# Sixteen-step transformer stack on one core: the last layer's two attentions and the cluster mix work several batches in different phases at once, and layer norm statistics are taken in the stage ahead

## The chip, the cores and the metric

The kernel runs on one core of one Trainium2 chip. The metric is the device time of one execution, in microseconds. Before the change the median of three runs is 6564.3 us (6562.81 to 6569.73).

## The reference, cut to what matters

A float32 tensor `x` of 16 sequences ("batches") of 256 tokens by 128 features passes through sixteen residual steps, `x = x + f(layernorm(x))`. The ones whose loops are rewritten:

```python
def _L3_attn_a_ref(x, q_w, kv_w, proj_w, proj_b):      # 16 heads of 8, windows of 32 tokens, one shared k and v
    q = x @ q_w.T
    k, v = split(x @ kv_w.T)                           # 8 features each
    attn = softmax(q_window @ k_window.T * 8 ** -0.5)  # per head and window: 32 x 32
    return (attn @ v_window) @ proj_w.T + proj_b

def _L3_attn_b_ref(x, Wq, bq, Wk, bk, Wv, bv, Wo, bo, g1, be1, W1, b1, W2, b2, g2, be2):
    q, k, v = heads(Wq, bq), heads(Wk, bk), heads(Wv, bv)
    qn, kn = elu(q) / norm(elu(q)), elu(k) / norm(elu(k))
    ctx = qn @ (kn.T @ v) / sqrt(8)                    # per head: an 8 x 8 state
    attn_out = layernorm(ctx @ Wo + bo + x, g1, be1)
    return layernorm(gelu(attn_out @ W1 + b1) @ W2 + b2 + attn_out, g2, be2)

def _L2_ffn_ref(x, ...):                               # used twice; its last part is the "mix"
    tile_idx = ...                                     # one of 64 rows of a table, for each token
    comp = tanh(gelu(x @ compress_w1 + compress_b1) @ compress_w2 + compress_b2)
    hh = relu(comp[:, 0:1] * w1a[tile_idx] + comp[:, 1:2] * w1b[tile_idx] + b1[tile_idx])
    mag = sum(hh * w2[tile_idx]) + b2[tile_idx]
    return layernorm(x + mag * directions[tile_idx] * output_scale) * norm_gamma + norm_beta
```

The order of the sixteen steps is: l0_attn_a, l0_ffn, l0_attn_b, l0_ffn, l1_attn_a, l1_ffn, l1_attn_b, l1_ffn, l2_attn_a, l2_ffn, l2_attn_b, l2_ffn, l3_attn_a, l3_ffn, l3_attn_b, l3_ffn.

## The kernel before, in words

`X` (the residual, 32 tiles of 128 tokens by 128) and `XNT` (the layer norm's output, features on the partitions) stay in SBUF. Each step is one or more blocks; all engines meet at the end of a block. Inside a block every engine runs its own program in order, and the programs wait for one another by counting semaphores (`wait_ge`, `then_inc`). A wait stops everything that is queued behind it on its engine. `drain()` makes VectorE wait for its own earlier writes.

Every step begins with `layer_norm`: VectorE takes `bn_stats` of all 32 tiles (line 193), combines them (lines 196 to 205), ScalarE takes a root, and then rows are scaled (line 216), turned by TensorE (line 240) and copied to `XNT` by ScalarE (line 265). Nothing else goes on in the block while the statistics are taken.

The attentions and the mix loop over pairs of batches, and each engine does phase after phase, both batches of the pair in each phase:

- `l3_attn_a` (lines 1385 to 1548): ScalarE copies the batch's slice of XNT (L1484); TensorE projects k and q (L1425, L1426); VectorE repeats the slice four times (L1515) for the product that gives v (L1431); VectorE masks v (L1521) and makes sixteen masked copies of k, one for each head (L1526); TensorE makes the scores (L1442); VectorE takes the maximum and subtracts it (L1533, L1535); ScalarE takes exp (L1493); VectorE sums, inverts and scales the probabilities (L1539, L1541, L1543); TensorE turns them (L1450), ScalarE copies them out (L1497), TensorE multiplies by v (L1459), and output copies (L1501, L1505), a second turn (L1466) and the last projection (L1468, L1473) follow; VectorE adds to X (L1548).
- `l3_attn_b` (lines 1168 to 1382): the same kind of chain: projection (L1224), bias and elu on VectorE with exp on ScalarE (L1332 to L1341), norms (L1343 to L1352, the root at L1295), the state (L1235, L1357), context (L1242), output projection on y1 (L1245 to L1252), first normalising (L830, L833, L1317, L1321, with a power on GpSimd), turn (L1259), the wide layer (L1266) with gelu (L1311), the second projection on y2 (L1270 to L1276), second normalising and the add to X (L1321 to L1382).
- the mix of `l2_ffn` (lines 2590 to 2701): ScalarE copies the one-hot rows (L2635), TensorE turns them (L2608) and starts the compression (L2609), ScalarE copies and takes gelu (L2639, L2643), TensorE picks the table's rows (L2615) and compresses (L2617, L2622), ScalarE takes tanh (L2647), and VectorE does all the rest (L2671 to L2701). ScalarE starts the next pair only when VectorE has added the last one to X (the semaphore `done`).

In `load_all` (lines 99 to 124) the first block ends only when six DMAs that fill `slots_x` in HBM with zeros have landed. In `sparse_experts` rows go out to HBM and come back by indirect DMAs on GpSimd's queue (L551, L559), and VectorE adds each returned tile to X (L492).

## Time and profile before

| | |
|---|---|
| median of three runs | 6564.3 us (6562.81 to 6569.73) |
| the profiled execution's own time | 6556.34 us |
| its span, first to last instruction | 6554.4 us |
| TensorE busy (matmul) | 3941.5 us, 60% |
| VectorE busy | 3888.1 us, 59% |
| ScalarE busy | 2334.7 us, 36% |
| GpSimd busy | 1684.8 us, 26% |
| mean granted TensorE clock | 0.78 of full speed |
| DMA | 26 GB/s over the span |

Busy is the share of the span in which an engine executes something; a granted clock of 0.50 is 1.2 GHz and 1.00 is 2.4 GHz, and a value between is a stretch that had both. No engine is near full, so the time lies in the waits of one engine for another, and those must be read stage by stage.

### The profile page before, as it was taken

The page shows a single profiled execution, that of the slowest core. Times are in us where ns is not written, and L with a number is a line of the kernel's source. Part 1 is how long each engine was busy: PE and PEld are TensorE (multiplying, and loading weights), DVE is VectorE, ACT ScalarE, POOL GpSimd, SP SyncE. Part 2 cuts the span into 40 slices and gives each one's busy share as a digit, 9 for nine tenths or more (in the row PEclk, how much of TensorE's full clock was granted, in tenths as well). Part 3 has the DMA queues.
Part 4 walks back from the last instruction along what each step waited for, and adds up shares of the span by engine and source line. Part 5 has one row for each costly group of instructions (what it writes and reads, how often), then busy time and mean ns, then how long its engine had stood idle before and what let it go on. Part 6 is the DMA issues. An engine that isn't in the chain of part 4 may idle for free. (4 is left out here: it accounts for less than half of the span.)

```text
span 6554.4 us, 78028 instructions
## 1 busy us (share of the span) xinstructions
PE 3941.5 (60%) x21844; PEld 2462.1 (38%) x21844; DVE 3888.1 (59%) x7406; ACT 2334.7 (36%) x4114; POOL 1684.8 (26%) x1639
## 2 busy tenths in 40 slices
PE   5756539366734688445666634888536647456474
PEld 3555429122223233231222222444324446444364
DVE  3334644599963777437888865555656635455354
ACT  2322214355512477224544432333322224233242
POOL 0043023455523355232433320000000041200402
PEclk8767659688867899676878865999756679777798
DMA  2012002000002222030000000000000011100111
GB/s 78 1 53 69 0 23 82 30 0 0 0 4 66 85 88 64 4 95 12 0 0 0 0 2 17 0 0 0 1 3 0 1 42 41 42 0 2 42 39 49
DMA packets 224792, 170.38 MB, mean 26 GB/s; under 512 B 27371, under 2 KB 211538, under 8 KB 223650
## 3 DMA queue, kind: packets, MB, share of 16 engines
q1 hardware_dynamic: 204066, 125.44, 6.5%
q0 software_dynamic: 20480, 41.98, 2.2%
q8 instruction: 114, 1.87, 0.1%
q14 instruction: 132, 1.08, 0.1%
HBM read 92.02 MB, written 74.45 MB: 25 GB/s over the span
## 5 line engine op out<-in xcount | busy, mean ns | idle before, releaser
L1630 POOL TENSOR_TENSOR XN<-s_l_attn_a_h,LOG 128x512 f32<-128x512 f32 x512 | 641.9, 1275 | 770.7 <-DVE s_l_attn_a_h L1670 754.2
L1670 DVE TENSOR_TENSOR_SCAN s_l_attn_a_h<-s_l_attn_a_da,XN 128x512 f32<-128x512 f32 x512 | 598.4, 1210 | 138.7 <-ACT s_l_attn_a_da L1615 98.5
L1606 PE MATMUL s_l_attn_a_y_ps<-XN,c_ident 128*128 128x512 f32 x1024 | 588.2, 703 | 24.4 <-DVE s_l_attn_a_y L1882 15.0
L613 PE MATMUL s_l_ffn_ffn_down<-down,s_l_ffn_ffn_hid 128*128 x2944 | 425.0, 285 | 206.6 <-DVE s_l_ffn_ffn_hid L485 184.1
L1615 ACT ACTIVATE s_l_attn_a_da<-s_l_attn_a_delta,s_l_attn_a_a 128x510 f32<-128x510 f32 x512 | 353.3, 690 | 526.9 <-DVE s_l_attn_a_h L1670 526.4
L559 POOL DMA_INDIRECT s_l_ffn_ffn_back<-slots_y,s_l_ffn_ffn_slots x320 | 303.0, 947 | 911.9 <-DMA slots_y<-PICK 617.3
L613 PEld LDWEIGHTS s_l_ffn_ffn_down<-down,s_l_ffn_ffn_hid 128*128 128x128 f32 x2944 | 362.3, 192 | 255.5 <-issue 253.8
L472 DVE COPY s_l_ffn_ffn_xt<-s_l_ffn_ffn_turned 128x128 f32<-128x128 f32 x416 | 121.0, 291 | 549.0 <-PE s_l_ffn_ffn_turned L594 547.2
L1585 PE MATMUL s_l_attn_a_spread<-s_l_attn_a_parts,s_l_attn_a_pick 96*128 96x512 bf16 x512 | 182.0, 442 | 388.7 <-DVE XN L1661 237.6
L605 PE MATMUL s_l_ffn_ffn_up<-s_l_ffn_ffn_xt,s_l_ffn_ffn_own_w 128*128 128x128 f32 x2944 | 410.7, 281 | 8.1 <-DVE s_l_ffn_ffn_own_w L405 4.8
L229 POOL COPY XN<-s_l_ffn_ln_rows 128x512 f32 x64 | 40.9, 638 | 1455.0 <-DVE s_l_ffn_ln_rows L216 1455.0
L551 POOL DMA_INDIRECT slots_x<-XN,s_l_ffn_ffn_slots x320 | 313.1, 978 | 390.1 <-DVE s_l_ffn_ffn_slots L449 294.4
L3154 DVE TENSOR_REDUCE s_l_attn_b_top<-s_l_attn_b_m_ps 128x2 f32<-128x512 f32 x512 | 330.0, 687 | 89.7 <-PE s_l_attn_b_m_ps L2860 85.6
L605 PEld LDWEIGHTS s_l_ffn_ffn_up<-s_l_ffn_ffn_xt,s_l_ffn_ffn_own_w 128*128 128x128 f32 x2944 | 370.3, 196 | 17.4 <-issue 11.2
L1606 PEld LDWEIGHTS s_l_attn_a_y_ps<-XN,c_ident 128*128 128x128 f32 x1024 | 224.6, 226 | 286.9 <-issue 235.7
L1661 DVE TENSOR_TENSOR XN<-s_l_attn_a_dx,s_l_attn_a_spread 128x1024 f32<-128x1024 f32 x256 | 306.0, 1195 | 6.4 <-PE s_l_attn_a_spread L1585 3.7
L3024 ACT ACTIVATE s_l_attn_b_e<-s_l_attn_b_s_ps 128x512 f32<-128x512 f32 x512 | 284.8, 604 | 40.1 <-PE s_l_attn_b_s_ps L2873 33.6
L594 PE MATMUL s_l_ffn_ffn_turned<-c_ident,XNT 128*128 128x128 f32 x416 | 115.5, 281 | 277.2 <-DMA XNT<-slots_x 277.2
L535 ACT ACTIVATE s_l_ffn_ffn_silu<-s_l_ffn_ffn_shifted_a 128x512 f32<-128x512 f32 x160 | 100.8, 630 | 482.0 <-DVE s_l_ffn_ffn_shifted_a L480 482.0
L1585 PEld LDWEIGHTS s_l_attn_a_spread<-s_l_attn_a_parts,s_l_attn_a_pick 96*128 96x128 bf16 x512 | 37.9, 102 | 615.2 <-DVE XN L1661 386.7
L539 ACT ACTIVATE s_l_ffn_ffn_hid<-s_l_ffn_ffn_up 128x512 f32<-128x512 f32 (+1 forms) x256 | 132.5, 518 | 346.8 <-PE s_l_ffn_ffn_up L605 346.1
L492 DVE SCALAR_TENSOR_TENSOR X<-s_l_ffn_ffn_back,s_l_ffn_ffn_gates,X 128x128 f32<-128x128 f32 x320 | 111.5, 350 | 204.3 <-DMA s_l_ffn_ffn_back<-slots_y,s_l_ffn_ffn_slots 198.3
(629 smaller groups left out, 8785.9 us busy)
## 6 DMA issues: line engine op xcount, KB each, us to landing
XNT<-slots_x SPq DMA_DIRECT2D x32, 640.0 KB, 6.0
slots_y<-LOG SPq DMA_DIRECT2D x16, 640.0 KB, 4.3
slots_y<-PICK SPq DMA_DIRECT2D x16, 640.0 KB, 4.3
s_l_attn_b_qr<-s_l_attn_b_q_rows SPq DMA_DIRECT2D x64, 144.0 KB
s_l_attn_b_kr<-s_l_attn_b_k_rows SPq DMA_DIRECT2D x64, 144.0 KB
XNT<-slots_x SPq DMA_DIRECT2D x8, 768.0 KB, 6.1
slots_x<-XN,s_l_ffn_ffn_slots POOLq DMA_INDIRECT x320, 2.2
s_l_ffn_ffn_back<-slots_y,s_l_ffn_ffn_slots POOLq DMA_INDIRECT x320, 2.5
```

Source lines behind the costliest of these rows:

```text
L551: nc.gpsimd.indirect_dma_start(k.slots_x[h][0:NH * P, :], bass.IndirectOffsetOnAxis(slots[:, c, t:t + 1], 0), k.XN[:, t, :], None).then_in ...
L559: nc.gpsimd.indirect_dma_start(back[:, n % 8, :], None, k.slots_y[h][0:NH * P, :], bass.IndirectOffsetOnAxis(slots[:, c, t:t + 1], 0)).the ...
L605: last = nc.tensor.matmul(out[:, c % chunks, :], own_w1[j % 3][:, c * P:(c + 1) * P], xt[j % 3][:], start=True, stop=True)
L613: last = nc.tensor.matmul(down[j % 2][:], hid[j % 3][:, c, :], w2[:, bass.ds(first + c * D, D)], start=(c == 0), stop=(c == chunks - 1))
L1585: last = self.nc.tensor.matmul(self.spread[:, i, :], self.pick[:, i * NST + n:i * NST + n + 1].to_broadcast([96, P]), self.parts[par][:], ...
L1606: last = self.nc.tensor.matmul(self.y_ps[:, i, :], self.k.ident[:], self.hc[n % 2][:, i, :], start=(n == 0), stop=(n == NST - 1))
L1615: self.nc.scalar.activation(self.da[:, i, :, 1:], self.delta[par][:, i, :].rearrange("p (b t) -> p b t", b=BPG)[:, :, 1:], ACT.Exp, scale= ...
L1630: self.nc.gpsimd.tensor_tensor(self.hc[n % 2][:, i, :], self.h[n % 2][:, i, :], self.c_rows[n % 2], ALU.mult).then_inc(self.hc_ready, 1)
L1661: self.nc.vector.tensor_tensor(self.u[n % 2], self.dx[par][:], b, ALU.mult).then_inc(self.u_ready, 1)
L1670: self.nc.vector.tensor_tensor_scan(self.h[n % 2][:, i, :], self.da[:, i, :, :].rearrange("p b t -> p (b t)"), self.u[n % 2][:, i, :], 0.0 ...
L3024: nc.scalar.activation(e[h][:], s_ps[BANK[n * H + h]][:], ACT.Exp, scale=HD ** -0.5).then_inc(e_ready, 1)
L3154: nc.vector.tensor_reduce(top[n % 2][:, :, h % 2, h // 2], m_ps[BANK[n * H + h]][:], AX.X, ALU.max).then_inc(max_ready, 1)
```

## The change

- `l3_attn_a`: one batch in each step instead of two, and in a step each engine works on up to four batches in different phases: batch i+2 is projected and its keys masked, batch i+1 is scored, shifted and exponentiated, batch i is turned, multiplied by v and turned back, batch i-1 is projected out and added. Each phase has a PSUM bank of its own. Eight of the sixteen masked key copies move to ScalarE; the four repeated copies move to GpSimd; probabilities are no longer scaled, the 128x256 output is divided instead (and ScalarE's copy of it goes away). A few steps ahead of the loop and behind it are written out (19 steps in all).
- `l3_attn_b`: a step does the first half (to the context) of one pair and the second half (from the output projection) of the pair before it, interleaved on each engine; 9 steps, the first and the last half empty. The residual's slice is copied once more (`xr`). `hid_ps` and `proj` are single banks or bank pairs shared by the two batches.
- The mix: front buffers in a ring of four; ScalarE waits for `rows_used` (VectorE's last read of the ring slot, four batches back) instead of `done`. The table is laid out by GpSimd with zeros so that one 128-row product picks each tile's rows.
- Statistics: `bn_stats` of a tile is taken right after its add to X in l0_attn_a, l0_attn_b, l2_attn_b and the three expert steps; the eight layer norms behind those steps skip line 193.
- Load: ten smaller fills, and the block no longer waits for them; GpSimd waits ahead of the first scatter.

```diff
@@ load_all
+                for first in range(0, 40, fill_tiles):          # fill_tiles = 8
+                    ...
+                    sp.dma_start(dst, ...).then_inc(k.slots_filled, 16)
-            sp.wait_ge(loaded, n + 16 + 6 * 16)
+            sp.wait_ge(loaded, n + 16)
+def take_stats(nc, dve, k, first, count):
+    dve.drain()
+    for t in range(count):
+        nc.vector.bn_stats(flat(k.stats[:, bass.ds(first + t, 1), :]), tile(k.X, first + t))
@@ layer_norm
+            if not stats_taken:
+                for t in range(TILES):
+                    nc.vector.bn_stats(stats[:, t, :], k.X[:, t, :])
+                dve.drain()
@@ sparse_experts, combine
+                if c == choices - 1:
+                    dve.drain()
+                    nc.vector.bn_stats(k.stats[:, t, :], k.X[:, t, :])
@@ sparse_experts, gpsimd
+            pool.wait_ge(k.slots_filled, k.fills)
@@ l0_attn_a and l0_attn_b, after each pair; l2_attn_b, after each group of four tiles
+                take_stats(nc, dve, k, pair * (2 * TPB), 2 * TPB)
@@ l3_attn_b, tensor
+            def step(a, b):
+                project(a, 0)
+                first_out(b, 0); first_out(b + 1, 1)
+                project(a + 1, 1)
+                turn_rows(b, 0); turn_rows(b + 1, 1)
+                go_up(b, 0)
+                turn_and_add_up(a, 0)
+                go_down(b, 0)
+                turn_and_add_up(a + 1, 1)
+                go_up(b + 1, 1)
+                apply_state(a, 0); apply_state(a + 1, 1)
+                go_down(b + 1, 1)
@@ l3_attn_b, vector
+            def step(a, b):
+                add_bias(a, 0)
+                variance(b, 0, 0, y1_ready); variance(b + 1, 1, 0, y1_ready)
+                add_bias(a + 1, 1)
+                normalise(b, 0, 0); normalise(b + 1, 1, 0)
+                square(a, 0); square(a + 1, 1); scale(a, 0); scale(a + 1, 1)
+                mask_state(a, 0); mask_state(a + 1, 1)
+                variance(b, 0, 1, y2_ready); variance(b + 1, 1, 1, y2_ready)
+                finish(b, 0); finish(b + 1, 1)
@@ l3_attn_b, scalar
+            def step(a, b):
+                keep_x(a, 0); keep_x(a + 1, 1); exponents(a, 0); exponents(a + 1, 1)
+                keep_rows(b, 0); keep_rows(b + 1, 1)
+                roots(a, 0); roots(a + 1, 1)
+                middle(b, 0)
+                keep_qt(a, 0); keep_qt(a + 1, 1); keep_residual(a, 0); keep_residual(a + 1, 1)
+                middle(b + 1, 1)
+                keep_ctx(a, 0); keep_ctx(a + 1, 1)
@@ l3_attn_a
+            tensor: turn_probs(i), project(i+2), project_out(i-1), score(i+1), mix(i), project_v(i+1), turn_out(i)
+            scalar: copy pt(i), keep_kq(i+2) with 8 key copies, keep_x(i+3), exp(i+1), copy ot(i)
+            vector: add_up(i), mask_keys(i+2) (8 copies), add_out(i-1), shift(i+1), divide(i), keep_v(i+1)
+            gpsimd: repeat(u+1) after v_up(u)
@@ l2_ffn mix
+        RING = 4
-                    act.wait_ge(done, u + 1)
+                        act.wait_ge(rows_used, u + 1)
-                        last = nc.tensor.matmul(row_ps[m][:, t, 0:TW], pt[m][r:r + NT, :], w["L2f_table"][r:r + NT, :], start=True, stop=True)
+                            last = nc.tensor.matmul(row_ps[m][:, t, 0:TW], pt[m][:], table[:, t, :], start=True, stop=True)
```

(The `step` lists of l3_attn_a are written here as one line for each engine; in l3_attn_b the conditions that leave out a or b in the first and last step are left out.)

## Rows read from the trace of the kernel before

**Rows 1.** Windows of five loops: length, busy us of each engine, clock, DMA, GB/s.

```profile
3897.00:4048.00 151.00, 59.89 (x208) 35.50 (x208) 76.35 (x304) 38.11 (x80) 11.38 (x16) 0.50 0.00 0
4754.00:4905.00 151.00, 56.57 (x208) 32.67 (x208) 76.68 (x304) 38.10 (x80) 11.35 (x16) 0.52 0.01 2
4926.00:5204.00 278.00, 175.38 (x1856) 116.38 (x1856) 175.50 (x432) 71.21 (x120) 0.00 (x0) 0.70 0.00 0
5412.00:5500.00 88.00, 62.99 (x518) 59.09 (x518) 45.24 (x84) 36.47 (x63) 0.00 (x0) 1.00 0.12 33
5733.00:6038.00 305.00, 179.40 (x864) 134.15 (x864) 152.60 (x416) 97.31 (x184) 22.40 (x33) 0.77 0.00 0
```

**Rows 2.** Timeline of l3_attn_a, one pair: start, length, engine, line, [idle before, releaser].

```profile
4968.88 8.48 DVE L1526 TENSOR_SCALAR s_l_attn_a_keys<-s_l_attn_a_kk,s_l_attn_a_c_head_of_row 128x256 f32<-128x256 f32 x32
4973.31 3.43 PE L1442 MATMUL s_l_attn_a_big_a<-s_l_attn_a_keys,s_l_attn_a_q 128*32 128x512 f32 x16 [4.80 <-DVE s_l_attn_a_keys L1526]
...
4977.51 1.92 PE L1442 MATMUL s_l_attn_a_big_a<-s_l_attn_a_keys,s_l_attn_a_q 128*32 128x512 f32 x16 [0.77 <-DVE s_l_attn_a_keys L1526]
...
4979.83 1.06 ACT L1493 ACTIVATE s_l_attn_a_p<-s_l_attn_a_p 128x1024 f32<-128x1024 f32 x1 [10.64 <-DVE s_l_attn_a_p L1535]
...
4985.14 1.97 PE L1450 MATMUL s_l_attn_a_big_b<-c_ident,s_l_attn_a_p 128*128 128x128 f32 x8 [5.71 <-DVE s_l_attn_a_p L1543]
...
4987.14 1.01 ACT L1497 COPY s_l_attn_a_pt<-s_l_attn_a_big_b 128x1024 f32<-128x1024 f32 x1 [3.82 <-PE s_l_attn_a_big_b L1450]
```

**Rows 3.** Groups by line, VectorE in l3_attn_a's loop: busy us, mean ns, idle before.

```profile
L1543 DVE TENSOR_TENSOR s_l_attn_a_p<-s_l_attn_a_p,s_l_attn_a_den 128x1024 f32<-128x1024 f32 x16 | 19.6, 1225 | 1.2
...
L1515 DVE COPY s_l_attn_a_xrep<-s_l_attn_a_xg 128x256 f32<-128x256 f32 x64 | 13.6, 286 | 5.8 <-ACT s_l_attn_a_xg L1484 5.2 <-issue 0.6
```

**Rows 4.** Timeline of l3_attn_b, one pair.

```profile
5807.45 0.49 DVE L830 BATCH_NORM_STATS2 s_l_attn_b_stats<-s_l_attn_b_late 128x6 f32<-128x128 f32 x2 [3.72 <-PE s_l_attn_b_late L1276]
...
5829.77 0.50 DVE L830 BATCH_NORM_STATS2 s_l_attn_b_stats<-s_l_attn_b_late 128x6 f32<-128x128 f32 x2 [4.00 <-PE s_l_attn_b_late L1252]
...
5840.18 0.50 DVE L830 BATCH_NORM_STATS2 s_l_attn_b_stats<-s_l_attn_b_late 128x6 f32<-128x128 f32 x2 [6.85 <-PE s_l_attn_b_late L1276]
...
5841.05 1.70 ACT L1311 ACTIVATE s_l_attn_b_hid<-s_l_attn_b_proj,s_l_attn_b_L3b_b 128x256 f32<-128x256 f32 x4 [2.62 <-PE s_l_attn_b_proj L1266]
...
5844.96 0.49 DVE L830 BATCH_NORM_STATS2 s_l_attn_b_stats<-s_l_attn_b_late 128x6 f32<-128x128 f32 x2 [3.72 <-PE s_l_attn_b_late L1276]
```

**Rows 5.** Timeline of the first mix, VectorE, first pair and start of the second.

```profile
3905.62 0.29 DVE L2671 TENSOR_TENSOR s_l_ffn_mix_sp<-s_l_ffn_mix_row_ps,s_l_ffn_mix_comp 128x32 f32<-128x32 f32 x2 [14.01 <-ACT s_l_ffn_mix_comp L2647]
...
3917.49 0.42 DVE L2701 TENSOR_TENSOR X<-X,s_l_ffn_mix_y 128x256 f32 x1
...
3924.55 0.29 DVE L2671 TENSOR_TENSOR s_l_ffn_mix_sp<-s_l_ffn_mix_row_ps,s_l_ffn_mix_comp 128x32 f32<-128x32 f32 x2 [6.63 <-ACT s_l_ffn_mix_comp L2647]
```

**Rows 6.** Timeline: statistics, and what VectorE does where they will be taken.

```profile
4905.36 6.29 DVE L193 BATCH_NORM_STATS2 s_l_attn_a_ln_stats<-X 128x6 f32<-128x128 f32 x32 [0.32 <-PEq L47]
...
253.94 0.96 DVE L962 TENSOR_TENSOR s_l_attn_a_qkv<-s_l_attn_a_proj,s_l_attn_a_L0a_bqkv 128x768 f32<-128x768 f32 x1 [1.06 <-PE s_l_attn_a_proj L880]
...
628.67 0.35 DVE L492 SCALAR_TENSOR_TENSOR X<-s_l_ffn_ffn_back,s_l_ffn_ffn_gates,X 128x128 f32<-128x128 f32 x1 [0.96 <-DMA s_l_ffn_ffn_back<-slots_y,s_l_ffn_ffn_slots]
...
4609.85 1.21 DVE L2405 TENSOR_TENSOR s_l_attn_b_swap<-s_l_attn_b_sw_ps,s_l_attn_b_c_sin 64x1024 f32<-64x1024 f32 x1
```

**Rows 7.** Timeline of the load block: the fills' issue, the next issue.

```profile
5.42 15.99 SPq L117 DMA_DIRECT2D slots_x<-PICK  x6
26.50 0.34 SPq L138 DMA_DIRECT2D up<-in_L_ffn_w  x1
```

**Rows 8.** Groups by line in layer norms, with and without GpSimd's copy beside them.

```profile
L216 DVE TENSOR_SCALAR s_l_ffn_ln_rows<-X,s_l_ffn_ln_meanvar,s_l_ffn_ln_rstd 128x128 f32 x32 | 10.4, 386 | 6.2 <-ACTq L260 5.5 <-issue 0.6
...
L216 DVE TENSOR_SCALAR s_l_attn_a_ln_rows<-X,s_l_attn_a_ln_meanvar,s_l_attn_a_ln_rstd 128x128 f32 x32 | 8.7, 342 | 1.7 <-ACTq L260 1.2 <-issue 0.5
...
L229 POOL COPY XN<-s_l_ffn_ln_rows 128x512 f32 x8 | 5.1, 642 | 323.2 <-DVE s_l_ffn_ln_rows L216 323.2
```

More of the change, by code:

```diff
@@ L1191, in l3_attn_b @@
[L1191 to L1194 removed]
+        proj, hid_ps = s.ps("proj", [P, TPB, 512]), s.ps("hid_ps", [P, CH, SEQ])
+        mid, late = s.two_ps("mid", [P, 512]), s.two_ps("late", [P, 512])
@@ L1200, in l3_attn_b, with over_phases, since @@
         block = s.block()
+        def over_phases(engine, step):
+            step(0, None)
+            with engine.Fori(0, PAIRS - 1) as pair:
+                step(pair * 2 + 2, pair * 2)
+            step(None, BATCH - 2)
+        def since(engine, sem, count):
+            if not isinstance(count, int) or count > 0:
+                engine.wait_ge(sem, count)
         @block.gpsimd
@@ new lines, in l3_attn_a, with has, over_batches @@
+        turned_o, ot_ready, y_up, added = s.sem("turned_o"), s.sem("ot_ready"), s.sem("y_up"), s.sem("added")
+        xrep_ready, v_up, vals_ready = s.sem("xrep_ready"), s.sem("v_up"), s.sem("vals_ready")
+        block = s.block()
+        def has(u):
+            return not isinstance(u, int) or 0 <= u < BATCH
+        def over_batches(engine, step):
+            for i in range(-2, 1):
+                step(i, i % 2)
+            with engine.Fori(0, (BATCH - 4) // 2) as pair:
+                step(pair * 2 + 1, 1)
+                step(pair * 2 + 2, 0)
+            for i in range(BATCH - 3, BATCH + 1):
+                step(i, i % 2)
@@ new lines, in score @@
+            def score(u, m):
+                since(pe, shifted, u)
+                pe.wait_ge(q_ready, u + 1)
+                pe.wait_ge(act_keys, u + 1)
+                pe.wait_ge(dve_keys, u + 1)
+                for t in range(TPB):
+                    for i in range(WPT):
+                        n = t * WPT + i
+                        last = nc.tensor.matmul(s_ps[i * WIN:(i + 1) * WIN, t, :], q[m][:, n * WIN:(n + 1) * WIN],
+                                                keys[m][:, n, :, :].rearrange("p h u -> p (h u)"), start=True, stop=True)
+                last.then_inc(scored, 1)
@@ new lines, in _, with repeat @@
+            pe.wait_ge(loaded, 16 * len(names))
+            over_batches(pe, step)
+        @block.gpsimd
+        def _(pool):
+            def repeat(u):
+                since(pool, v_up, u)
+                for h in range(HB):
+                    last = nc.gpsimd.tensor_copy(xrep[:, :, h, :], k.XNT[:, bass.ds(u * SEQ, SEQ)].rearrange("p (n u) -> p n u", u=WIN))
+                last.then_inc(xrep_ready, 1)
+            repeat(0)
+            with pool.Fori(0, BATCH - 1) as u:
+                repeat(u + 1)
@@ L2651, in _ @@
             nc.gpsimd.memset(minus[:], -0.5)
+            nc.gpsimd.memset(table[:], 0.0)
+            pool.drain()
+            pool.wait_ge(loaded, 16 * len(names))
+            for t in range(TPB):
+                r = t * NT
+                last = nc.gpsimd.tensor_copy(table[r:r + NT, t, :], w["L2f_table"][r:r + NT, :])
+            last.then_inc(table_ready, 1)
             pool.drain()
@@ L3367, in build @@
             STEPS[step](nc, k, f"s{n}_{step}")
+            k.stats_taken = step not in ("l3_attn_a", "l2_ffn", "l3_attn_b", "l1_attn_a", "l1_attn_b", "l2_attn_a")
             later = [p for p in plan[n + 1:] if p in experts]
```

812 lines of the change are left out of this document (427 added, 385 removed).

## The prediction, made before the changed kernel was run

> **What bounds the kernel now.** I read the totals first: no engine is busy for more than 60% of the span, so no engine's work is the limit. The chain of waits says little, as it only follows the last expert step. So I cut the span into the loops that the change touches and read windows of them, then one pair of each loop in the timeline. The reader is to see three things. In both mixes VectorE is the busiest engine with 76 us of 151, at a clock of 0.50 [rows 1]. In l3_attn_a TensorE and VectorE are each busy 175 of 278 us, the clock at 0.70; in l3_attn_b 179 and 153 of 305, at 0.77 [rows 1]. And in the timeline these take turns: ScalarE waits 10.64 us for the shift, TensorE 4.80 for the keys and 5.71 for the probabilities [rows 2]; in l3_attn_b VectorE waits 4.00 us for y1, then 6.85 and 3.72 for y2 [rows 4]; in the mix 6.63 us for tanh [rows 5]. All are latencies of a chain with two batches at the same place in it, and they are what several phases at once can fill. The eight layer norms hold VectorE for 6.29 us with nothing beside [rows 6].
>
> **l3_attn_a.** A pair takes 278/8 = 34.8 us, a batch 17.4 [rows 1]. VectorE per batch afterwards: eight key copies at 8.48/32 = 0.265 us = 2.1 (sixteen before) [rows 2]; maximum and subtraction, each of 1024 elements like the 1225 ns row, with overlap and drain 2.5; the sum of 1024 and the reciprocal 1.7; the scaling of 1225 ns goes and a 256-element one of about 0.45 comes; masked v and the add 0.45 each; the repeats (4 x 286 ns, overlapped 0.85) leave [rows 3]. Sum 7.7 us. TensorE at 2.4 GHz: score 1.9 (3.4 at 1.2 GHz), turning eight blocks about 1.2 (the row has 1.97 behind a long wait) [rows 2]; k and q 0.8, v 1.9, times v 1.1, output and second turn 1.2, from the same pair of the timeline: 8.2 us. ScalarE: probabilities out 1.01, exp 1.06 [rows 2], k, q, x and output copies 1.3, table load 0.6 (one in two steps), and eight key copies. A 256-column activation with a per-partition operand is not there as a copy; the nearest is gelu with a bias, four in 1.70 us, 0.43 apart [rows 4]. Bounds are 0.27 and 0.57 apart (2.1 to 4.5 us for eight); I take 0.42, 3.4 us. Sum 7.4 us.
>
> No sum is the step, because the order closes a ring. With t = 0 where exp(i) ends: TensorE turns to 1.4, ScalarE copies out to 2.5 and hands over k at 2.9; VectorE, idle since 1.8, masks keys to 5.1 and adds out to 5.6; TensorE has meanwhile made k, q and the output and ends the score of i+1 at 5.0; the shift runs to 8.1; exp 8.3 to 9.35, and the ring is closed. Product by v (6.1), v's projection (8.0) and divide (8.6) lie beside it. ScalarE's key copies end at 6.7 (7.9 at the upper bound) and are hidden by the shift. So 9.4 us, with the table load and loop ends 9.8. What is late next is VectorE's wait for k, 1.1 us. Fifteen such steps are 147, two steps of filling 15, the last real one 5.5, the one behind it 2: 170 us. The clock will not be full everywhere, 4 us. 278 becomes 174: **-104** (bounds: 9.2 us a step gives -113; 11.5 us, TensorE mostly at 1.2 GHz with 12.6 us of work in some steps, gives -78).
>
> The four repeats go to GpSimd, which has nothing else and works a step ahead, so they are off the ring. Against them stands what a copy on GpSimd does to VectorE beside it: rows scaled in a layer norm take 386 ns beside GpSimd's 642 ns copies and 342 without [rows 8]. On eight key copies that is at most 0.35 us a step, inside the 4 us above and its bound. The Trainium skill ("SBUF — State Buffer", Who interferes with whom) says of this that a VectorE instruction in a two-port mode and a GpSimd instruction exclude each other for their whole length. If key copies fell under it and always came second, four copies of half of 642 ns would stop VectorE for 1.3 us in each of 16 batches, 21 us; the rows show 44 ns, so I don't count it.
>
> **l3_attn_b.** One pair takes 37.5 us (5807.45 to 5844.96) [rows 4]. VectorE's waits in it are 3.72 + 4.00 + 6.85 and 2.0 of small ones, so its work with drains is 21 us. The new step has all that work once. I follow it from the end of the squares, about 11.7 us into a step (two biases 3.8, two variances 1.9, normalising 1.4, two squares 4.3): ScalarE's second root, table load, four gelus of 0.43 [rows 4] take 3.4 us; TensorE, whose order puts the second batch's turn and state behind go_down(b), finishes them at 5.0, so VectorE, which had 3.0 us of work, waits 2.0. Then go_up of the second batch, its gelus behind the qt and residual copies (7.7), two apply_state, go_down (1.7): y2 of the second batch at 10.2, against VectorE ready at 6.4: a wait of 3.8. Then a variance and two finishes, 5.4. Sum 11.7 + 10.2 + 5.4 = 27.3, and the next step's projection is hidden by the finishes. I take 27.7 for the clock. The first step is a's chain alone, 19.5 us, the last b's alone, 22. 19.5 + 22 + 7 x 27.7 = 235 against 305: **-70** (bounds: 26 us a step -82; 31 us -46). The extra copy `xr` and three table loads a step are in ScalarE's 14 us of 27.7. TensorE has 16.6 us at 2.4 GHz. The single `hid_ps` makes go_up(b+1) wait for the first gelus, which the order does anyway.
>
> **The mixes.** VectorE is busy without a gap from 3905.62 to 3917.91, 12.3 us, then waits 6.63 us [rows 5]. With the ring, ScalarE may start a pair when VectorE has read the rows two pairs back, at least 12 us ahead of need, and its chain takes 8.5 us. So the wait goes; VectorE's own 12.1 us (the second pair has 12.0) is late next. 8.6 (first front) + 8 x 12.1 + 2.5 (table layout on GpSimd, loop) = 108 against 151 [rows 1]: **-86** for both (bounds: no lead at all 0; -90). The clock of 0.50 hides in the lead as well.
>
> **Statistics.** 8 x 6.29 us go, less 0.1 each, as the ScalarE table load of 1.28 us beside them now ends last: -49.6 [rows 6]. What comes: 32 bn_stats at 0.197 us again, in other places. In l0_attn_a four and a drain, 0.95 us, against an idle 1.06 [rows 6]: 0.1 a pair, and 0.95 behind the last: 1.8; in l0_attn_b the idle time there is longer, 1. In l2_attn_b nothing stands between the add and the next work, which is on the path (L2405 has no idle time before it) [rows 6]: 8 x 0.95 = 7.6, more than the 6.2 that its successor's norm gives back. In the experts' tail each add waits 0.96 us for a returned tile [rows 6] and the new 0.3 us fits, except the last: 0.35 in each of four; in l1_ffn, where every add has one, I put 1.5 in each of two. The last l3_ffn takes them for nothing. Together +14.8, net **-35** (bounds -25 to -44).
>
> **Load.** The fills' issue on SP's queue, 16 us for the same bytes, stays, and the wait from 21.4 to 26.5 goes [rows 7]: **-4.6** (bounds 0 to -5). Weights issued next lie behind the same transfers, but are wanted 20 us later.
>
> **Sum.** 104 + 70 + 86 + 35 + 5 = 300 off the profiled execution's 6556.3 = 6256. The runs shown have a median 8 us over that execution, so 6264; for handshakes that my schedules leave out I add 6: **6270 us**.
>
> **Rivals.** (1) *The steps are longer than the hand schedule*: TensorE stays at 1.2 GHz for much of the two attentions. For it speaks that the clock is 0.70 and 0.77 now with TensorE busy 63% and 59%; against it that an expert loop with TensorE busy 72% and no wait over 2 us has 1.00 [rows 1]. Price: l3_attn_a steps of 12.6 us (TensorE's work at 1.2 GHz) 15 x 2.8 = 42 more, l3_attn_b steps of 33 us 7 x 5.3 = 37 more: 6350 us. The Trainium skill ("TensorE: Matmul & The Clock Gate", HAM oscillation) says that waits between bursts throw the array back to the lower clock. The waits that I leave in the step are under 3 us where they were 4.8 to 5.7, and by that rule, too, the higher clock is the likelier. (2) *The mix's front doesn't run ahead*, because ScalarE's queue waits for tanh of this pair before it copies the next: 8 chains of 8.5 us still fit into 12.1, so little speaks for it; 86 less gain, 6356. (3) *More than I count*: steps at 9.2 and 26, the norms' -44: 6240, or near 6215 if the copies by ScalarE cost 0.27. (4) *Slower than before*: the in-order queues close the rings so that no two phases overlap, l3_attn_a above all, where a step has one batch and four engines pass it on. One batch's chain alone is 26 us there: 19 x 26 = 494, +216; l3_attn_b 8 x 41.5 = 332, +27; mixes -86, norms -35, load -5: 6680. It decides once a step of l3_attn_a is longer than some 27 us, three times my ring, and nothing in the rows needs that. (5) *It doesn't do what it says* (the norms still take statistics, the loop still in step): within 0.2%, 13 us.
>
> **How the numbers follow.** Forecast 62%, its own range 6235 to 6310; rival 1 and 2 together 22%; rival 3 13%; rival 4 2%; rival 5 1%. The 8-in-10 range takes in rival 1's and 2's price on the slow side and, on the fast side, rival 3's with a little of the unlisted gains: 6205 to 6360. About 0.2% is what a measurement of this kernel can tell from no change. Faster 97%, same 1%, slower 2%.
>
> **What would show it.** Right: loops of about 174 and 235 us and two of 108; ScalarE's exp in l3_attn_a released every 9.8 us; VectorE in the mix with no wait for tanh after the first; a wait of VectorE for y2 near 4 us; line 193 in eight norms only; the clock over 0.85 in both attentions; VectorE's idle time before L2405 gone into bn_stats. Wrong: a step of l3_attn_a over 11.5 us, TensorE the engine without gaps in it, or ScalarE's key copies beyond the end of the shift.

## The result, and the profile after

The changed kernel takes **6264.6 us** (median of four runs, 6253.8 to 6268.7) against 6566.7 for the kernel before in the same session (6562.8 to 6569.7): a ratio of **0.9538**, 95% interval 0.9521 to 0.9554. Its profiled execution took 6263.55 us with a span of 6261.6, 292.8 us less than the one before. The forecast was 6270.

The windows of the loops in the changed kernel, in the order of the two mixes, l3_attn_a and l3_attn_b (columns as in [rows 1]: after the length come the busy times of TensorE, its weight loads, VectorE, ScalarE and GpSimd, then the granted clock):

```profile
3859.50:3964.40 104.90, 59.65 (x208) 39.74 (x208) 76.55 (x304) 27.45 (x72) 12.05 (x18) 0.58 0.00 0
4671.90:4776.80 104.90, 58.40 (x208) 39.27 (x208) 76.48 (x304) 27.48 (x72) 12.02 (x18) 0.60 0.00 0
4798.00:4974.00 176.00, 155.46 (x1856) 108.46 (x1856) 115.69 (x240) 100.74 (x225) 22.86 (x64) 0.81 0.00 1
5496.20:5745.20 249.00, 187.99 (x864) 135.22 (x864) 151.00 (x416) 100.60 (x199) 22.40 (x33) 0.84 0.00 0
```

Against [rows 1] VectorE does the same work in less time in the mixes and in l3_attn_b: it is busy 73% of a mix instead of 51%. In l3_attn_a it has 60 us less to do (115.7 against 175.5), of which 30 came to ScalarE (100.7 against 71.2) and 23 to GpSimd, and TensorE is busy 88% of the loop instead of 63%. The clock came out at 0.81 and 0.84 in the attentions.

To place every microsecond I cut each kernel at the instruction in each norm with which VectorE completes the variance, just ahead of the root (line 205 before, 216 in the changed kernel), so a stage is a step and the statistics of the norm behind it. Microseconds, worked out from the timelines:

```
stage (ends at the next norm's root)     before   after   difference
load and first norm                        35.1    32.5     -2.6
l0_attn_a                                 295.0   282.9    -12.1
l0_attn_b                                 243.6   238.5     -5.1
l0_ffn, twice                       313.8+316.6 307.8+309.2  -13.4
l1_ffn, twice                       262.1+260.9 254.8+256.0  -12.2
l2_attn_b                                 630.4   627.0     -3.4
l1_attn_a, l1_attn_b, l2_attn_a          2098.1  2102.7     +4.6
l2_ffn, twice                       230.9+226.3 187.7+185.5  -84.0
l3_attn_a                                 299.2   197.9   -101.3
l3_attn_b                                 326.9   270.1    -56.8
l3_ffn, twice                       507.1+508.5 500.3+508.8   -6.5
```

One step of l3_attn_a in the timeline of the changed kernel (columns as in [rows 2]):

```profile
4862.95 1.06 ACT L1637 ACTIVATE s_l_attn_a_p<-s_l_attn_a_p 128x1024 f32<-128x1024 f32 x1 [1.84 <-DVE s_l_attn_a_p L1660]
...
4864.06 1.97 PE L1524 MATMUL s_l_attn_a_t_ps<-c_ident,s_l_attn_a_p 128*128 128x128 f32 x8 [0.26 <-ACT s_l_attn_a_p L1637]
...
4866.68 0.85 PE L1533 MATMUL s_l_attn_a_kq_ps<-s_l_attn_a_xg,s_l_attn_a_L3a_wq 128*128 128x256 f32 x2
...
4867.97 2.19 DVE L1651 TENSOR_SCALAR s_l_attn_a_keys<-s_l_attn_a_kk,s_l_attn_a_c_head_of_row 128x256 f32<-128x256 f32 x8 [2.28 <-ACT s_l_attn_a_kk L1620]
...
4868.72 1.93 PE L1552 MATMUL s_l_attn_a_s_ps<-s_l_attn_a_keys,s_l_attn_a_q 128*32 128x512 f32 x16
...
4870.72 1.23 DVE L1658 TENSOR_REDUCE s_l_attn_a_top<-s_l_attn_a_s_ps 128x32 f32<-128x1024 f32 x1 [0.22 <-PE s_l_attn_a_s_ps L1552]
...
4873.27 1.06 ACT L1637 ACTIVATE s_l_attn_a_p<-s_l_attn_a_p 128x1024 f32<-128x1024 f32 x1 [1.83 <-DVE s_l_attn_a_p L1660]
```

From one exp to the next is 10.32 us (10.25 later in the loop). The shift is released by the score and not by VectorE's own masks. The score is released by nothing, it stands behind TensorE's own turn, projection and output. Windows inside this step, of the same kernel, show at which clock (the last column but two):

```profile
4864.00:4866.10 2.10, 2.04 (x9) 2.04 (x10) 1.57 (x2) 0.30 (x3) 0.41 (x2) 0.50 0.00 0
4866.10:4867.60 1.50, 1.50 (x5) 0.87 (x5) 0.00 (x0) 1.01 (x2) 0.00 (x0) 0.64 0.00 0
4867.60:4873.20 5.60, 5.54 (x102) 3.73 (x102) 4.93 (x12) 3.84 (x11) 0.00 (x0) 1.00 0.00 0
4873.20:4874.30 1.10, 0.41 (x2) 0.20 (x2) 0.70 (x3) 1.03 (x2) 0.99 (x3) 0.87 0.00 0
```

The turn and most of k and q run at 1.2 GHz, the rest at 2.4 GHz; the fall comes in the only stretch of the step in which TensorE is mostly idle (0.41 of 1.10 us busy). All steps of the loop but one have such a stretch at 1.2 GHz. The one without it, between the second exp and the third, is 1.6 us shorter than its successor, with the same instructions:

```profile
4822.80:4831.62 8.82, 8.01 (x116) 5.59 (x116) 7.21 (x16) 6.11 (x15) 1.43 (x4) 1.00 0.01 2
4831.62:4842.07 10.45, 9.61 (x116) 6.77 (x116) 7.21 (x16) 6.20 (x14) 1.43 (x4) 0.84 0.01 2
```

VectorE in l3_attn_b, its wait for y2 of the second batch in two full steps, 27.55 us apart, and for y2 of the first batch in the last step; TensorE's wide layer of that step stands ahead of it:

```profile
5602.17 0.50 DVE L845 BATCH_NORM_STATS2 s_l_attn_b_stats<-s_l_attn_b_late 128x6 f32<-128x128 f32 x2 [4.38 <-PE s_l_attn_b_late L1282]
...
5629.72 0.50 DVE L845 BATCH_NORM_STATS2 s_l_attn_b_stats<-s_l_attn_b_late 128x6 f32<-128x128 f32 x2 [4.38 <-PE s_l_attn_b_late L1282]
...
5725.46 3.73 PE L1271 MATMUL s_l_attn_b_hid_ps<-s_l_attn_b_at,s_l_attn_b_L3b_w 128*128 128x256 f32 x8
...
5734.65 0.50 DVE L845 BATCH_NORM_STATS2 s_l_attn_b_stats<-s_l_attn_b_late 128x6 f32<-128x128 f32 x2 [9.72 <-PE s_l_attn_b_late L1282]
```

VectorE in the first mix, the first instruction of the second and of the third pair (the same as in [rows 5], where it waits 6.63 us for tanh):

```profile
3880.26 0.28 DVE L2834 TENSOR_TENSOR s_l_ffn_mix_sp<-s_l_ffn_mix_row_ps,s_l_ffn_mix_comp 128x32 f32<-128x32 f32 x2
...
3892.38 0.29 DVE L2834 TENSOR_TENSOR s_l_ffn_mix_sp<-s_l_ffn_mix_row_ps,s_l_ffn_mix_comp 128x32 f32<-128x32 f32 x2 [0.18 <-issue]
```

The load block, to be compared with [rows 7]; of the 5.1 us between the fills' issue and the next one 0.45 are left:

```profile
5.42 16.14 SPq L118 DMA_DIRECT2D slots_x<-PICK  x10
22.01 1.42 SPq L140 DMA_DIRECT2D up<-in_L_ffn_w  x1
23.48 1.24 SPq L140 DMA_DIRECT2D down<-in_L_ffn_w  x1
25.11 0.34 SPq L197 DMA_DIRECT2D s_l_attn_a_L0a_wqkv<-in_L0a_wqkv  x1
```

### The profile page after: what moved, and what is told of

Read it like the earlier page. It is cut to its first block and busy times, and to the rows that moved or that the text cites. A ratio compares the mean times of both kernels' runs of the same rounds, so it can differ in the third digit from the quotient of the medians.

```text
span 6261.6 us, 78605 instructions
## 1 busy us (share of the span) xinstructions
PE 3935.5 (63%) x21844; PEld 2470.7 (39%) x21844; DVE 3852.3 (62%) x7246; ACT 2346.4 (37%) x4218; POOL 1709.6 (27%) x1709
```

## The experiments

They were measured in four sessions, each with the kernel before beside them. It takes 6566 us in two of them (the record numbers their chips 15 and 6) and 6739 in the other two (numbered 2 and 6). In the changed kernels all of the difference is in the six expert stages (l0_ffn 347 us there against 308), and every other stage agrees within the spread given below. What makes those stages longer isn't shown; the number 6 stands beside both times. So kernels are compared by their ratio to the kernel before in the same session, and by stages, each read from one profiled execution. A ratio of 0.001 is 6.6 us. Stages with unchanged code spread between profiles: l0_attn_a 282.8 to 288.8, l2_attn_a 876 to 894, l3_attn_b 264.5 to 270.1 (ten profiles, mean 266.7).

**All statistics back in the norms.**

```diff
-            k.stats_taken = step not in ("l3_attn_a", "l2_ffn", ...)
+            k.stats_taken = False
-                take_stats(nc, dve, k, ...)      # and the bn_stats in combine
```

> The changed kernel (6264.6 us) with every layer norm taking its own statistics again and none taken in a stage ahead; all else as changed. By the terms of my sum the statistics are worth 35 us: 6300 us. Rival, from the stages compared after the run: the eight stages ahead of these norms got 53 us shorter and three stages whose code is the same 5 us longer, so 48 to 53: 6313 to 6318 us. If the 5 us of the three stages (l1_attn_a, l1_attn_b, l2_attn_a) belong to the statistics too, they must fall back to their times before (1.2, 2.4 and 1.0 us less); if not, they stay.

Ratio 0.9625 (0.9611 to 0.9638): 57 us more than the changed kernel. By stages, against those of the next three kernels (same session) that keep the stage as changed: l0_attn_a +10 (against one of them, and 6 to 12 against the spread), l0_attn_b +5, the five expert stages +5, +5, +9, +5 and +6, l2_attn_b +5, together 50. My 35 is out. l1_attn_a, l1_attn_b and l2_attn_a take 661.4, 563.1 and 876.5 us, 2101.0 together, against 2102.7 in the changed kernel and 2098.1 before. The 4.6 us between those two did not go away with the statistics, and they are smaller than the spread of l2_attn_a alone.

**Statistics of l2_attn_b alone back in the norm.**

```diff
-                take_stats(nc, dve, k, g * GT, GT)
```

> The changed kernel with the statistics of l2_attn_b alone moved back to the norm behind it. By my term they cost 7.6 us in the loop (8 times 0.95, nothing beside) against 6.2 in the norm: the stage gets 1.4 us shorter, 6263 us. Rival: VectorE's next wait for TensorE's swapped product takes the 0.95 us in (6.18 us before, 5.23 after), and only the last of eight is on the path: the stage gets 4 to 5 us longer, 6269 us. The times are within the measurement's bound of each other, so the stage in the profile decides: group period 75.05 us with the statistics out, 75.1 with them in, if the rival holds; 76.0 with them in by my term.

Ratio 0.9554 (0.9538 to 0.9570), which can't tell; the stage took 632.5 us against 626.6 to 627.6 in the others: 5.4 more. The rival holds by the stage. Groups by line over the stage, in the kernel before and then in the changed one, show where the 8 us of statistics went (last column: idle before the line, and what ended it):

```profile
L2405 DVE TENSOR_TENSOR s_l_attn_b_swap<-s_l_attn_b_sw_ps,s_l_attn_b_c_sin 64x1024 f32<-64x1024 f32 x64 | 77.8, 1216 | 156.2 <-PE s_l_attn_b_sw_ps L2315 156.2
```

```profile
L2555 DVE TENSOR_TENSOR s_l_attn_b_swap<-s_l_attn_b_sw_ps,s_l_attn_b_c_sin 64x1024 f32<-64x1024 f32 x64 | 77.8, 1215 | 149.0 <-PE s_l_attn_b_sw_ps L2465 149.0
...
L167 DVE BATCH_NORM_STATS2 LOG<-X (+1 forms) x32 | 8.0, 291 | 1.4 <-issue 1.2
```

In the kernel before, the first L2405 behind the add to X has no wait ([rows 6]), but the next one has 6.18 us. Over the stage 7.2 us of these waits vanished against 8.0 us of new work.

**Statistics of l0_attn_a alone back in the norm, and the same taken twice.**

```diff
 # e7: in l0_attn_a only
-                take_stats(nc, dve, k, pair * (2 * TPB), 2 * TPB)
 # e8: in l0_attn_a only
+                take_stats(nc, dve, k, pair * (2 * TPB), 2 * TPB)
```

> The changed kernel with the statistics of the first attention (l0_attn_a) alone moved back to the norm behind it. By my term: 6.2 more in the norm, 1.8 less in the loop, 6269 us. Rival: the 12.1 us that this stage gained are mostly the clock, which was granted in another rhythm over its eight pairs once each pair was a little longer (30.0, 33.5 and 35.4 us in turn at 0.89, 0.80 and 0.76, where before 33.1 and 35.2 took turns); then the old rhythm comes back and the stage loses some 12 us: 6276 us.

> The changed kernel with the four statistics behind each pair of l0_attn_a taken twice (the second time is waste). If a statistic is simply work on the path, each pair gets 0.87 to 0.95 us longer and nothing else changes: 7 to 7.6 us, 6272 us. Rival: pair lengths follow the clock, and a shift of 0.9 us moves which pairs get the high one: the 30.0, 33.5, 35.4 us rhythm changes to another, and the stage moves by several us in either direction beside the 7: anywhere from 6260 to 6285 us, with at least two pairs over 1.5 us away from where they were.

Without them the ratio is 0.9562 (0.9549 to 0.9575) and the stage 292.9 us. With them twice it is 0.9530 (0.9514 to 0.9545) and the stage **268.0 us**: 0.76 us of waste work in each pair (VectorE busy 13.61 us against 12.85) made the stage 15 us shorter. The ratio of the whole kernel is too coarse to confirm the 15 us: it is 5 us below the changed kernel's, and the intervals overlap. Windows of three pairs of the changed kernel, then of two of the kernel with the statistics twice:

```profile
183.84:213.87 30.03, 21.44 (x97) 15.57 (x96) 12.85 (x25) 11.43 (x21) 0.00 (x0) 0.89 0.00 0
213.87:247.41 33.54, 24.95 (x97) 17.89 (x96) 12.85 (x24) 11.43 (x21) 0.00 (x0) 0.80 0.00 0
247.41:282.84 35.43, 26.84 (x97) 19.50 (x96) 12.86 (x25) 11.43 (x21) 0.00 (x0) 0.76 0.00 0
```

```profile
174.67:205.43 30.76, 21.43 (x97) 15.58 (x96) 13.61 (x29) 11.43 (x21) 0.00 (x0) 0.89 0.00 0
205.43:236.20 30.77, 21.44 (x97) 15.58 (x96) 13.61 (x29) 11.43 (x21) 0.00 (x0) 0.89 0.00 0
```

The same 97 matmuls take 21.4 or 26.8 us. In the changed kernel the granted clock goes through a rhythm over three pairs; with 0.76 us more work in each pair, all seven distances from pair to pair are 30.76 to 30.79 us, and the clock 0.89. Without the statistics five of the seven distances are 33 and 35 us again, as in the kernel before. So the rivals hold on the mechanism in both runs. On the size they don't: without them the stage is 4 to 10 us longer than in the kernels that have them once, not 12, and with them twice it gained more than "several us".

**The mix in step again.**

```diff
-                        act.wait_ge(rows_used, u + 1)
+                        act.wait_ge(done, u + 1)       # done: VectorE's add to X
```

> The changed kernel with one edit in both mixes: ScalarE waits for the add of the batch two back (as before the change) instead of for VectorE's last read of the ring slot four back. Ring, banks and the padded table stay. If the lead is the whole of the gain, each mix gives its 42 us back: two VectorE waits of 6 to 7 us for tanh a pair again, 6348 us. Rival: the front also got shorter or longer by the padded table and the banks of its own; then each mix lands elsewhere than at 151 us, by 8 times the difference of a front (0.4 us of TensorE in a pair: 3 us a mix).

6346.8 us, 0.9664 (0.9650 to 0.9679): 82 more. The two l2_ffn stages took 231.4 and 226.8 us, those of the kernel before 230.9 and 226.3. The lead is the whole gain; ring buffers and the padded table alone give nothing.

**Score first in l3_attn_a; score and shift first.**

```diff
 # TensorE, both
+                if has(i + 1):
+                    score(i + 1, 1 - par)
                 if has(i):
                     turn_probs(i, par)
 ...
-                if has(i + 1):
-                    score(i + 1, 1 - par)
 # VectorE, the second kernel only: shift(i + 1) ahead of add_up(i)
```

> The changed kernel with one edit in l3_attn_a: TensorE makes the scores of batch i+1 first in a step, ahead of turning the probabilities of batch i, of the projection of i+2 and of the output of i-1. Theory: a step is 10.3 us because TensorE's own queue is on the ring (turn 1.97, k and q 1.9, output 1.3, score 1.93), where I had put VectorE's masks there; with the score out of the way VectorE's shift starts as soon as the add is done, at 6.55 instead of 6.7 behind the end of exp, so this alone gives little, 0 to 0.2 us a step, and turning may be held back by 0.9 us behind the score: 6262 to 6278 us. Rival: TensorE alone is the ring, and a step shrinks by the score's 1.9 us: 6234 us.

> The same with VectorE's order changed as well: it shifts the scores of i+1 first, then adds up i and masks the keys of i+2. The shift then runs beside exp of i and the turn, and the ring through the keys is cut: the longest of the engines' own sums is left. TensorE 8.5 us at 2.4 GHz, VectorE 7.7, ScalarE 8.4 with its table loads: a step of 8.8 to 9.2 us instead of 10.3, 17 to 24 us less, 6244 us. Rival: ScalarE's queue (copy out, eight key copies, then exp of i+1) still takes a whole step behind the turn, so the step stays over 10 us: 6262 us; against both, steps may get longer if the clock falls in the new gaps.

The first: 6281.1 us, 0.9571 (0.9558 to 0.9584), and the stage took 220.8 us against 197.9: worse than both theories. The second: 6265.6 us, 0.9547 (0.9532 to 0.9562), stage 202.9. Two steps of the second, one behind the other:

```profile
4853.04:4863.01 9.97, 8.08 (x117) 5.53 (x116) 7.13 (x17) 6.11 (x16) 1.86 (x4) 1.00 0.00 0
4863.01:4875.37 12.36, 10.83 (x117) 6.56 (x116) 7.95 (x20) 6.10 (x15) 1.83 (x4) 0.72 0.01 1
```

Its steps are 8.0 to 10.0 us at full clock and 10.7 to 12.5 at 0.72 to 0.84. The long ones are those with the lower clock. That the new order shortens the ring at full clock isn't shown: the one full-clock step of the old order is 8.82. In the first kernel, the score stands between exp and the turn, and there it took up to 3.64 us at 1.2 GHz (1.92 at 2.4).

**The second batch earlier in l3_attn_b.**

```diff
                     turn_and_add_up(a, 0)
+                    turn_and_add_up(a + 1, 1)
+                    go_up(b + 1, 1)
                     go_down(b, 0)
-                    turn_and_add_up(a + 1, 1)
-                    go_up(b + 1, 1)
 # ScalarE: middle(b + 1, 1) ahead of keep_residual
```

> The changed kernel with one edit in l3_attn_b: TensorE turns and adds up the second batch of pair a right behind the first, and makes the wide layer of the second batch of pair b before the second projection of the first; ScalarE takes the second batch's gelu before the residual copies. Theory: VectorE's two waits in a step (2.22 us for the second state, 4.38 us for y2) are set by TensorE's and ScalarE's order, not by their work. The state comes 2 us earlier and y2 1.5 to 2.5 us earlier: a step of 25 us instead of 27.55 and 2 us off the last one, 6242 us (a range of 6236 to 6252). Rival: the wait for y2 is the length of the chain through the gelus, and only moves to the first y2: 6262 us.

6271.6 us, 0.9551 (0.9538 to 0.9564), stage 272.5 us against a mean of 266.7 and at most 270.1: the rival holds, and the stage got a little longer still. VectorE's waits for y2 in a step of this kernel:

```profile
5602.37 0.49 DVE L845 BATCH_NORM_STATS2 s_l_attn_b_stats<-s_l_attn_b_late 128x6 f32<-128x128 f32 x2 [4.58 <-PE s_l_attn_b_late L1282]
...
5605.02 0.49 DVE L845 BATCH_NORM_STATS2 s_l_attn_b_stats<-s_l_attn_b_late 128x6 f32<-128x128 f32 x2 [1.59 <-PE s_l_attn_b_late L1282]
```

The wait of 4.38 us moved to the first batch (4.58), 1.59 came behind it, and most steps are 28.0 us instead of 27.55.

**TensorE's waits filled.** Ahead of a wait stand matrix products of no use. Their result is overwritten, and it goes to a PSUM bank that nobody reads then.

```diff
 # l3_attn_a: ahead of turn_out three, ahead of turn_probs one
+                    nc.tensor.matmul(t_ps[:, 0, 0:P], k.ident[:], w["L3a_wo"][:], start=True, stop=True)
 # l3_attn_b: ahead of turn_rows(b, 0) five of
+                        nc.tensor.matmul(ctx_ps[0], k.ident[:], w["L3b_w2"][:, 0:SEQ], start=True, stop=True)
 # l0_attn_a: ahead of the wait for unit five of (into h1_ps[0] two, ahead of mixed)
+                    nc.tensor.matmul(den_ps[0], k.ident[:], w["L0a_w2"][:, 0:SEQ], start=True, stop=True)
```

> The changed kernel with products of no use put into TensorE's waits in three stages (their result is overwritten): five of 256 columns ahead of the wait for normalised q and k in l0_attn_a and two ahead of the wait for the divided output there; five of 256 columns ahead of turning the rows in l3_attn_b; three of 128 columns ahead of the second turn and one ahead of turning the probabilities in l3_attn_a. Theory: these stages are longer than their schedules because TensorE comes back from each such wait at 1.2 GHz (0.50 granted while it turns the probabilities and makes k and q, 2 us of 10.3 lost in a step of l3_attn_a; 3 to 9 us at 0.50 behind the 4 us wait in l3_attn_b; half of l0_attn_a), so with the waits filled the clock is over 0.95 and the work behind them takes its time at 2.4 GHz: l3_attn_a 10.3 to 8.6 us a step (-25), l3_attn_b 27.6 to 26 (-12), l0_attn_a from 283 us to 250 (-30): about 6200 us. Rival: the clock falls for another reason, and the fill only adds its own time where it runs over a wait (at 1.2 GHz a filling is twice as long): 6265 to 6285 us.

**6222.2 us, 0.9471 (0.9457 to 0.9486)**, 42 less than the changed kernel. l3_attn_a takes 177.3 us (-20.6), l0_attn_a 265.7 (-19 against the mean of seven profiles, 284.7), l3_attn_b 266.2 (nothing). Two steps of l3_attn_a in this kernel, and its turn of the probabilities:

```profile
4860.39:4869.20 8.81, 8.77 (x126) 6.51 (x125) 7.20 (x16) 6.11 (x15) 1.44 (x4) 1.00 0.00 0
4869.20:4878.06 8.86, 8.80 (x126) 6.51 (x125) 7.21 (x16) 6.11 (x15) 1.44 (x4) 1.00 0.00 0
```

```profile
4870.41 1.04 PE L1530 MATMUL s_l_attn_a_t_ps<-c_ident,s_l_attn_a_p 128*128 128x128 f32 x8
```

A step is 8.84 us at a granted 1.00, as long as the one full-clock step of the changed kernel, and the turn takes 1.04 us instead of 1.97. So the clock was what held the ring at 10.3. In l3_attn_b the step stayed at 27.54 us, with its waits of 2.23 and 4.38 us. The filling did not hold the clock there. These are a step of the changed kernel, and a step of this one with its first wide layer, which takes 3.64 us against 1.89 for the second:

```profile
5602.17:5629.72 27.55, 21.25 (x108) 15.50 (x108) 18.80 (x52) 12.69 (x26) 2.79 (x4) 0.94 0.00 0
```

```profile
5534.88:5562.42 27.54, 23.69 (x120) 17.45 (x119) 18.78 (x54) 12.70 (x25) 2.79 (x4) 0.94 0.00 0
```

```profile
5542.69 3.64 PE L1275 MATMUL s_l_attn_b_hid_ps<-s_l_attn_b_at,s_l_attn_b_L3b_w 128*128 128x256 f32 x8
```

So this run doesn't tell what a full clock would give in l3_attn_b. It does show that its first wide layer isn't on the path: it took 3.25 us in the changed kernel, and 0.4 us more did not lengthen the step.

**The reordered l3_attn_a filled; in l3_attn_b the states last.**

```diff
 # l3_attn_a as in the second reordering, and five products ahead of turn_out
 # l3_attn_b
+                    go_down(b + 1, 1)
                     apply_state(a, 0)
                     apply_state(a + 1, 1)
-                    go_down(b + 1, 1)
```

> The changed kernel with the scores and the shift first in l3_attn_a, as in the run before that was no faster (steps of 8.0 us at full clock and of 12.4 us at 0.72 in turn), and five products of no use of 128 columns ahead of the second turn, where TensorE waits 1.5 us. In l3_attn_b, beside it, TensorE applies the states behind the second projection of the second batch instead of ahead of it. Theory for l3_attn_a: the reordering did shorten the ring, and the clock took it back; with the wait filled every step is near 8.6 us: the stage takes 175 us against 198, 24 less. Rival: steps over 10 us again. For l3_attn_b: y2 of the second batch comes 1.0 us earlier, 26.6 us a step and 7 less for the stage (266 is the middle of eight profiles with the same code, 264 to 270, so 259), or, if VectorE's chain sets the step, nothing. Both right: 6234 us; neither: 6265 us.

6269.9 us, 0.9545 (0.9532 to 0.9558). l3_attn_a: the clock is 1.00 in a window over two steps and they take 9.7 and 10.05 us in turn, the stage 191.2; at full clock the new order is worse than the old, 8.84. In the trace exp starts 3.07 us behind the end of its shift, since ScalarE's copies and key copies stand ahead of it, the queue that the rival of the second reordering named. In this order GpSimd's copies also meet VectorE's key masks:

```profile
4876.97 2.33 DVE L1656 TENSOR_SCALAR s_l_attn_a_keys<-s_l_attn_a_kk,s_l_attn_a_c_head_of_row 128x256 f32<-128x256 f32 x8 [0.15 <-issue]
...
4878.61 1.64 POOL L1611 COPY s_l_attn_a_xrep<-XNT 128x256 f32 x4 [8.39 <-PE s_l_attn_a_v_ps L1571]
```

Of its 128 masks 18 take 478 to 534 ns, all of them beside a copy, and no mask without a copy beside it takes more than 355; the copies beside masks take 403 to 560 ns against 395 to 402.

l3_attn_b: 275.5 us. Two steps of it:

```profile
5577.16:5608.56 31.40, 25.85 (x109) 18.00 (x108) 18.94 (x53) 12.70 (x25) 2.79 (x4) 0.78 0.00 0
5608.56:5635.24 26.68, 21.21 (x109) 15.33 (x108) 18.78 (x53) 12.70 (x25) 2.79 (x4) 0.94 0.00 0
```

The step of 26.6 us that I worked out is there (26.68, the wait for y2 3.52 instead of 4.38), so TensorE's order has a part in the step. But such steps come in turn with steps of 31.4 us at 0.78.

**Filled, with the statistics of l0_attn_a in the norm; and a third attention filled.**

```diff
 # e13: filled l0_attn_a and l3_attn_a, take_stats out of l0_attn_a
 # e14: filled l0_attn_a (6 and 2), l3_attn_a, and in l0_attn_b ten (and two, into mid) of
+                    nc.tensor.matmul(turned[0], k.ident[:], w["L0b_w"][:, 0:SEQ], start=True, stop=True)
```

> The kernel with filled waits, without the filling in l3_attn_b, and with the statistics of l0_attn_a taken in the norm behind it. It asks what they are worth when the clock holds. With the waits filled l0_attn_a took 265.7 us with the statistics in its loop. By my term (6.2 in the norm against 1.8 in the loop) it now takes 4.4 more: 270.1 us, and the whole kernel 4 us more than with them in. Rival, by the two unfilled runs (292.9 and 295.0 against 283 to 289): 8 to 12 us more, 274 to 278 us; then the rhythm of the clock isn't what made the difference. l3_attn_b without its filling keeps its 265 to 267 us if VectorE's chain sets that step, and gets longer if the filling did help. The time: 6224 us, by the rival 6232.

> The changed kernel with TensorE's waits filled in l3_attn_a as before, in l0_attn_a (six and two products of 256 columns instead of five and two), and new in l0_attn_b (ten ahead of the wait for normalised q and k, which is 8.7 us, two ahead of the wait for the normalised output); none in l3_attn_b. In l0_attn_b TensorE comes back from the 8.7 us wait at 0.50 and works 5.3 us so, on the path. Theory: with the clock held a pair of 27.35 us loses 2 to 3 us, the stage 16 to 24 of 238, and the kernel ends at 6200 us. Rival: the filling (4.3 us at 2.4 GHz, 8.6 at 1.2) doesn't hold the clock over a wait of that length, or VectorE's chain sets the pair: 6222 us as with the filled waits before.

The first: ratio 0.9478 (0.9465 to 0.9492), l0_attn_a 272.6 us against 265.7 and 266.9 with the statistics in. In the filled stage (clock 0.92 to 0.93 instead of 0.83) they are worth 6 to 7 us: between my 4.4 and the rival's 8. l3_attn_b without filling took 268.4. The second has the lowest ratio: **0.9456 (0.9443 to 0.9469)**, 54 us below the changed kernel at 6566 us for the kernel before, though its interval overlaps with that of the first filled kernel. Its l0_attn_b takes 218.7 us against 238.3. l0_attn_b in the changed kernel, then in this one:

```profile
623.20:861.70 238.50, 142.56 (x512) 99.09 (x512) 152.99 (x382) 63.61 (x106) 11.30 (x17) 0.67 0.01 3
```

```profile
647.70:866.40 218.70, 161.22 (x704) 117.66 (x704) 152.59 (x382) 63.32 (x105) 11.30 (x17) 0.86 0.01 3
```

TensorE executes 192 matmuls more there (the 96 products of no use, two instructions each), and the stage is 20 us shorter. The filling doesn't cover the wait: of its 8.7 us 4.4 are left, and in the pair read the clock still fell at its end, but it stayed low for 3.4 us instead of 10.2.

## Why the prediction was right, and where it was right by luck

The time was right (6264.6 against 6270), and no rival's time came. Most of the gain came by the mechanisms that the forecast names. That it was met within 6 us is luck: four gains were forecast too large, by 13, 3, 2 and 2 us, one too small by 15 to 18, and these cancel. The stages with unchanged code, 4.6 us longer, and the 6 us added for handshakes cancel as well.

- **l3_attn_a, -104: measured -101.** The windows before the first exp and behind the last are as worked out (14.4 and 7.8 us against 15 and 7.5). The fifteen steps took 153.8 us, not 147: 10.25 a step, not 9.8. The term that failed is TensorE's on the ring, the chain of waits that closes on itself once a step. I put the turn at 1.2 to 1.4 us and k and q at 0.8, and they took 1.97 and 1.9 (1.04 and 1.2 with the waits filled), since the clock is at 1.2 GHz just there. [Rows 2] had the 1.97, and I discounted it as the mark of a long wait. So VectorE's wait for k was 2.28 and not 1.1, and the score, not the masks, ends last. Filling the waits gave 8.84 against the schedule's 9.4: the schedule was even cautious, and what it left out was the clock.
- **l3_attn_b, -70: measured -57**, -60 by the mean of ten profiles. The full step was right (27.55 against 27.7, waits of 2.23 and 4.38 against 2.0 and 3.8). The ends were not. Cut at VectorE's first bias of a step (in the last at its first variance), the loop is 23.9 + 200.0 + 25.1 = 249 against 19.5 + 194 + 22 = 235. The first step ends for ScalarE at 20.1, but the next one's table load, copy and projection (3.8 us) have nothing beside them. Of the seven full steps five took 27.5 to 27.6; the first took 32.5 at a clock of 0.80 and the sixth 29.8 at 0.83, where the short ones have 0.94. And the last half ran at 1.2 GHz up to its first y2 (a wide layer 3.73 us against 1.89), with 9.72 us of VectorE waiting for it.
- **The mixes, -86: measured -84.** Pairs of 12.0 us without a wait, and undoing the lead alone gave all of it back.
- **Statistics, -35: measured -53**, and 50 when the experiment undid them. The six microseconds that a norm gives back were right (5 to 6 in most stages). What failed is the price of putting them in: in l2_attn_b I saw no idle time before the next instruction and called it the path (+7.6), and the wait one instruction further took it in (about +1). That is 7 us of the 18. In the two l1_ffn my 3.0 came out at nothing (-12.2 against two norms of 6.2). And l0_attn_a gained 12 for 4.4, of which 6 to 7 are the statistics' (measured with the waits filled); the rest is the clock's rhythm.
- **Load, -4.6: measured -2.6.** The wait went; the two issues behind the fills took 1.42 and 1.24 us instead of 0.34 and 0.43. Why isn't shown.
- The copies on GpSimd cost VectorE nothing visible: eight masks took 2.19 us against 8 x 0.265 = 2.12 before; GpSimd's copies (4863.0 to 4864.4) don't lie beside them. Where they did, in the reordered kernel, a mask took some 0.14 us longer, about once a step: inside the 0.35 us that I had allowed, and far from the 1.3 us of the worst case.
- **What would show it**: the clock over 0.85 failed (0.81, 0.84), the loop of l3_attn_b took 249 us and not about 235, and exp came every 10.25 us and not 9.8. The loops of 176 and 105 us, the wait near 4 us for y2 and the mix without a wait for tanh came. VectorE's idle time before L2405 did go into bn_stats (156.2 to 149.0), which means that they were not on the path: my sign to watch contradicted my own price.

Rival 1 was half right. In l3_attn_a the clock did stay at 1.2 GHz in part of nearly each step and cost 1.4 us a step (10.25 against 8.84), not 2.8.

The Trainium skill ("TensorE: Matmul & The Clock Gate", A second HAM failure mode: psum-queue depth-cycling) also tells of a kernel whose array goes to and fro between the two levels because of frequent short pauses between groups of matmuls. The steps above look like it: 0.7 us of idling in 1.1 us, and 3 us at 0.50 behind it. I had weighed only the case of long waits. That the cause is the same isn't shown.

Still open: which pattern of work and pauses makes the clock fall. In the second reordered l3_attn_a (score and shift first) the clock fell in a pause of 1.54 us at 4842 us, and did not in one of 1.55 us, with 0.34 more soon behind it, at 4853.
